# Moving the transpose of P behind the step's other queue entries, and loading wq in four column parts, in a causal attention plus mixture-of-experts kernel

## The reference

```
h = layernorm(x)
q, k, v = split(h @ W + b)            # W: 1024 x 3072
x = x + softmax(mask(q @ k.T / 32)) @ v
h = layernorm(x)
p = softmax(h @ router_w); keep the two largest of 8 as c
routed = sum_e c_e * (silu(h @ w1[e]) @ w2[e])
shared = sigmoid(h @ gate_w) * ((silu(h @ Wg) * (h @ Wu)) @ Wd)
x = x + routed + shared
```

## Time and profile before

| | us |
|---|---|
| median of 2 runs | 2761.55 |
| the two runs | 2738.25 and 2784.85 |
| profiled execution, its time | 2776.87 |
| its span on the slowest core (core 3) | 2775.0 |
| spans of the 8 cores | 2720.0 to 2775.0 |
| TensorE busy | 2249.7 (81%) |
| Vector busy | 729.1 (26%) |
| Scalar busy | 708.7 (26%) |
| Scalar idle until a load of xkv lands | 384.5 |
| Vector idle until a load of xkv lands | 349.5 |

### The profile page before, as it was taken

The page is one execution under the profiler, slowest core; times in us unless marked ns, Lnnn a source line. Parts: engine busy times, 40 slices in busy tenths (PEclk is TensorE's granted clock), DMA queues, the critical chain, the costliest instruction groups (busy, mean ns, idle before and its releaser), DMA issues.

```text
span 2775.0 us, 26258 instructions; the slowest of 8 cores (2720.0 to 2775.0 us)
## 1 busy us (share of the span) xinstructions
PE 2249.7 (81%) x9600; PEld 954.8 (34%) x9600; DVE 729.1 (26%) x945; ACT 708.7 (26%) x1256; POOL 58.7 (2%) x190
## 2 busy tenths in 40 slices
PE   2529699789779688696859346689999999999999
PEld 0203244233234233232323112234444444444444
DVE  3422332331342332323332311120211202202112
ACT  3212322332232333334342332212011021120110
POOL 0000000000000000000000000000000000000000
PEclk8769899787789889787978578899999999999999
DMA  6471320320230321303241323200311131113013
GB/s 144 103 111 37 76 58 14 79 58 29 57 76 25 73 76 37 79 29 80 56 95 29 70 44 53 46 0 1 59 33 31 31 61 31 31 31 61 1 31 121
DMA packets 204062, 149.70 MB, mean 54 GB/s; under 512 B 176160, under 2 KB 176288, under 8 KB 203936
## 3 DMA queue, kind: packets, MB, share of 16 engines
q1 hardware_dynamic: 189872, 101.88, 14.8%
q0 software_dynamic: 14064, 46.16, 10.6%
HBM read 142.79 MB, written 8.39 MB: 54 GB/s over the span
## 4 chain that ended last, share of the span: by engine, by line
PE 66%; DMA 10%; ACT 7%; DVE 6%; SPq 5%; issue 3%; DVEq 2%; ACTq 2%
PE pO L893 16%; PE sp L872 16%; PE pO L536 9%; PE pO L505 9%; DMA xb<-xkv 6%; PE pO L417 3%; SPq L226 3%; PE sp L348 3%; DMA xb<-xq 3%; PE sp L792 2%; PE sp L797 2%; DVEq L51 2%; ACTq L51 2%; PE pO L263 2%; ACT P L390 2%
## 5 line engine op out<-in xcount | busy, mean ns | idle before, releaser
L348 PE MATMUL sp<-K_sb,Q_sb 128*128 128x512 bf16 x1088 | 317.0, 458 | 163.5 <-ACT P L390 152.4
L872 PE MATMUL sp<-Q_sb,w 128*128 128x512 bf16 x2048 | 443.3, 379 | 0.0
L893 PE MATMUL pO<-w_sb,hb 128*128 128x512 bf16 x2048 | 443.3, 379 | 0.0
L902 DVE SCALAR_TENSOR_TENSOR O<-pO,c_sb,O 128x1024 f32<-128x1024 f32 x128 | 164.3, 1284 | 719.7 <-PE pO L893 719.7
L417 PE MATMUL pO<-V_sb,PTd 128*128 128x512 bf16 x1088 | 275.6, 411 | 67.9 <-DMA PTd<-P 67.9
L880 ACT ACTIVATE hb<-sp 128x1024 bf16<-128x1024 f32 x128 | 131.2, 1025 | 752.8 <-PE sp L872 752.8
L505 PE MATMUL pO<-xlnT,wkv_sb 128*128 128x512 bf16 x1024 | 247.1, 408 | 61.9 <-DMA xlnT<-xlnb 56.9
L872 PEld LDWEIGHTS sp<-Q_sb,w 128*128 128x128 bf16 x2048 | 200.4, 98 | 241.6
L893 PEld LDWEIGHTS pO<-w_sb,hb 128*128 128x128 bf16 x2048 | 200.4, 98 | 241.6
L536 PE MATMUL pO<-wkv_sb,xlnT 128*128 128x512 bf16 x1024 | 250.0, 401 | 0.0
L348 PEld LDWEIGHTS sp<-K_sb,Q_sb 128*128 128x128 bf16 x1088 | 119.5, 113 | 357.9 <-issue 299.8
(11 more groups left out here) (81 smaller groups left out, 1040.4 us busy)
## 6 DMA issues: line engine op xcount, KB each, us to landing
xb<-xkv SPq DMA_DIRECT2D x64, 512.0 KB, 4.6
xb<-xq SPq DMA_DIRECT2D x32, 512.0 KB, 4.2
w<-w1p POOLq DMA_DIRECT2D x8, 2048.0 KB, 16.2
w_sb<-w2p POOLq DMA_DIRECT2D x8, 2048.0 KB, 16.3
out<-O SPq DMA_DIRECT2D x16, 512.0 KB, 2.7
wkv_sb<-wkvh POOLq DMA_DIRECT2D x2, 2048.0 KB, 29.5
wgu<-wguh POOLq DMA_DIRECT2D x16, 256.0 KB, 5.7
wq_sb<-wqh POOLq DMA_DIRECT2D x1, 2048.0 KB, 21.9
```

Source lines behind the costliest of these rows:

```text
L348: p.emit("tensor", lambda e, t=t, h=h, qc=qc, j=j: e.matmul(sp[j][:, h * 512:h * 512 + 512], Q_sb[:, qc * 2048 + t * 128: qc * 2048 + t * ...
L872: p.emit("tensor", lambda e, e_i=e_i, th=th, fc=fc, dc=dc, nbq=nbq, jj=jj: e.matmul(sp[jj][:, nbq * 512:nbq * 512 + 512], w1_sb[e_i % 2][: ...
L893: p.emit("tensor", lambda e, th=th, tc=tc, fc=fc, nbq=nbq: e.matmul(pO[tc % 2][:, nbq * 512:nbq * 512 + 512], hb[th][:, fc * 1024 + tc * 1 ...
L902: p.emit("vector", lambda e, tl=tl, tc=tc, e_i=e_i: e.scalar_tensor_tensor(out=O[tl][:], in0=pO[tc % 2][:], scalar=c_sb[:, tl * 8 + e_i: t ...
```

## The change

Two edits.

The first is in the tile loop. `emit_PdmaT` of tile i is no longer emitted right after `emit_exp` of tile i, but in step i+1, ahead of that step's `emit_softmax`. Only SP's list is affected. For the last tile of a block it is emitted behind the loop and the AV before the last.

The second loads wq as four DMAs, each with 256 of the 1024 columns of all eight 128-row chunks, each with its own semaphore; column groups 2w and 2w+1 of `emit_qproj` wait for part w alone. In the program's list the DMA is 128x4x2048 elements before (pieces of 4096 bytes in SBUF, which holds bf16) and four times 128x8x256 after (pieces of 512 bytes); the two loads of wkv are 128x8x1024 (2048 bytes).

```diff
-    WQ = mk("WQ"); WKV = mk("WKV"); WV = mk("WV"); RG = mk("RG"); DW = mk("DW")
+    WQ = [mk(f"WQ{i}") for i in range(4)]; WKV = mk("WKV"); WV = mk("WV"); RG = mk("RG"); DW = mk("DW")
...
-    p.emit("gpsimd", lambda e: e.dma_start(out=wq_sb[:], in_=wqh, max_dma_last_dim=8192),
-           inc=WQ, inc_n=16)
-    lw_wq = WQ.n
+    for wqq in range(4):
+        p.emit("gpsimd", lambda e, wqq=wqq: e.dma_start(
+            out=wq_sb[:].rearrange("p (dc n) -> p dc n", dc=DC)[:, :, wqq * 256:wqq * 256 + 256],
+            in_=wqh.rearrange("p (dc n) -> p dc n", dc=DC)[:, :, wqq * 256:wqq * 256 + 256],
+            max_dma_last_dim=8192), inc=WQ[wqq], inc_n=16)
     emit_memsets()
...
     def emit_qproj(g, trd_wait):
         nonlocal u
-        p.wait("tensor", WQ, lw_wq)
...
         for qc in range(8):
+            p.wait("tensor", WQ[qc // 2], 16)
             p.wait("tensor", SC, pO_free_sc[u % 2])
...
                 t_av = emit_AV(at, ah, ar, apte)
                 emit_Ofin(at, ah, ar, t_av, asc)
+            if pend:
+                pt_, ph, pr, psc, _ = pend[-1]
+                v_pte = emit_PdmaT(pt_, ph, pr, psc)
+                pend[-1] = (pt_, ph, pr, psc, v_pte)
             v_nmnew = emit_softmax(t, halves, masked, r, t_qk, sc_exp_parity[r % 2])
             sc_exp = emit_exp(t, halves, r, v_nmnew)
             sc_exp_parity[r % 2] = sc_exp
-            v_pte = emit_PdmaT(t, halves, r, sc_exp)
-            pend.append((t, halves, r, sc_exp, v_pte))
+            pend.append((t, halves, r, sc_exp, None))
...
-        pt_, ph, pr, psc, v_pte = pend[-1]
+        pt_, ph, pr, psc, _ = pend[-1]
+        v_pte = emit_PdmaT(pt_, ph, pr, psc)
         while qidx < n_kv_items:
             run_item(items[qidx]); qidx += 1
```

## The result

The changed kernel takes 2568.31 us (median of 11 runs) against 2784.1 for the kernel before (10 runs beside it). The ratio is 0.9322, with a 95% interval from 0.9262 to 0.9381: 6.8% faster, some 187 us of the 2761.55 that the prediction started from.

What follows compares the result with a forecast made beforehand. Attention was taken as bound by a ring: in-order SP held loads of x behind P transposes waiting for exp. Gains 124 + 28 + 17 + 7 = 176, less 17 and 4, took 2761.55 to about 2605 us; range 2565 to 2665.

Steps and rivals of the forecast that it cites:

- The ring over the load: Attention blocks 0 to 4: earlier loads of x let two tiles take 15.4 us; 24.8 us a block, 124 in all.
- The sum: Gains of 124 (blocks 0 to 4), 28 (xq loads), 17 (block 5) and 7 (block 6): 176 us.
- my net: Whole kernel: 176 us less 17 and less 4, a gain of 155 to 156 us.
- 4 for wq: Start of kernel: loading wq in short pieces delays the first projection, a loss of 4 us.
- the tenth: 17 us taken off the 176 for kvt issues of 2.1 us and QK at the lower clock after a pause.
- rival A: Attention: denser matmuls hold the clock at 0.81, costing 140 us; net gain 16, 2745 us; chance 0.07 in either form.
- p3: Blocks 1 to 4: xq loads no longer behind a transpose; 8 us in blocks 1 to 3, 4 in block 4, 28 total.
- rival C: Attention steps: P issued late behind kvt holds up exp, 5.3 us a step; 2920 us, or 2840 with half; chance 0.02.
- Two marks: Signs of being right: xkv loads at 2% or less of the chain; Scalar's 384.5 us idle before L172 more than halved.
- B: Blocks 0 to 4: ring only partly opened, 9.7 us a tile, 84 us instead of 124; 2643 us; chance 0.19.
- D: SP's queue order does nothing, since loads wait for a free xb buffer; 2760 us; chance 0.04.
- the forecast: Whole kernel: the median becomes about 2605 us; chance 0.68.

Runs made afterwards that it cites:

- e4: Kernel before, wq in one DMA, transpose of P moved behind kvt but still ahead of the load: 2738.86 us against 2790.95.
- e9: e5 with three entries a step once the key tiles are done, so the p3 entries are spread as before: 2528.16 us, ratio 0.9153.
- e1: Changed kernel with wq back in one DMA, so only the transpose of P moved: 2558.4 us against 2790.95, ratio 0.929.
- e2: Kernel before with only wq loaded in four column parts, transposes of P as before: 2799.71 us against 2790.95.
- e5: e1 with each key load split from its sums, sums taken one step later, more entries a step: 2593.43 us, ratio 0.922.
- e3: Changed kernel with wq laid out by column part, so its four DMAs move 4096-byte pieces in place of 512: 2567.99 us.
- e7: The edits of e5 and e6 together: median 2566.11 us, ratio 0.9163.
- e10: The edits of e9 and e6 together: 2530.05 us, ratio 0.912.
- e8: e1 with blocks 5 and 6 keeping the old order of the transposes of P: 2611.48 us, ratio 0.932.
- e6: e1 with phase q's factors and normalisation of tile i-1 emitted ahead of the square of tile i: median 2573.88 us, ratio 0.9127.

## Why the prediction was right, and where it was off

*The ring over the load* was right in place and size. Two tiles in 15.4 us was predicted, 15.4 and 15.6 were measured; e4 shows that with the load behind P the ring stays, and e9 that it opens fully when the load gets a step's time before its sum is taken.

*The sum.* Cores 0, 1, 6 and 7 have no long stretch at 0.81 in either profile, so they show the change without that level of the clock. They became faster by 184.9, 183.1, 181.0 and 180.2 us (2722.0, 2734.8, 2720.0, 2733.8 before). That is 182 on the mean, where my net was 155 and my 176 less 4 for wq is 172. On core 0, from the issue of load 3 to the three loads ahead of the next block, blocks 0 to 4 take 135.7, 133.2, 121.4, 108.3 and 112.3 us before and 112.7, 100.7, 86.5, 73.7 and 82.7 after:

| block | gain in the sum | measured on core 0 |
|---|---|---|
| 0 | 24.8 | 23.0 |
| 1 | 32.8 | 32.5 |
| 2 | 32.8 | 34.9 |
| 3 | 32.8 | 34.6 |
| 4 | 28.8 | 29.6 |
| 5 | 17 | 17.5 |

For block 5 the stretch is from the three loads to the next three, 140.4 and 122.9 us. Block 6, from its first kvt to its last P, took 50.3 us before on core 3. On core 0 it took 49.0 (1357.82 to 1406.84) and takes 41.1 (1185.42 to 1226.47), a gain of 8 where the sum had 7. The terms are right within about 2 us each, and together they gave 180 where the sum had 176.

*The step that failed is the tenth.* I took 17 us off for slow kvt issues and for QK at the lower clock. The first doesn't show in the step times of the table, and the second was taken with the wrong sign: with fewer pauses QK ran slowly less often (302.0 to 257.3 us on core 0, in the lines above). Of the 27 us that the 155 is short of 182, this is 17, the terms are 4 and wq, as told below, up to 4; the last 2 stay open. No run shows a price for either of the two reasons that I gave for the tenth.

*The clock went in the other direction from rival A.* Cores 2 and 3, granted 0.81 for part of attention in the profile before (core 3 in the V projection of the earlier trace rows), gained 229.8 and 227.6 us, some 46 more than those four, and have no long stretch at 0.81 after. Core 5, at 0.81 before too, held it after for part of block 0 (0.81 over 310 to 400 us) and gained 187. That the ratio's 187 is above the 182 of the four cores fits this, but isn't shown by itself. So 0.81 came and went between executions on changing pairs of cores; e4 had it on cores 0, 1, 6 and 7. Denser attention alone doesn't bring it on: the profiles of the changed kernel and e1 are denser and have less of it. With one profile each it isn't shown that it became rarer, and what brings it on stays open. The Trainium skill's rule ("TensorE: Matmul & The Clock Gate", warning on the peak-current limiter), by which a whole die falls to 13/16 of the clock once three of its cores run dense matmuls, isn't what these profiles show: after the change all eight cores are dense in the expert stage, and each was granted 1.00 over 1827 to 2500 us.

*p3* behaved as worked out: tiles 5 and 7 are 18.8 us apart (538.99 to 557.83), 18.1 expected, 22.1 before.

*wq.* A loss of 4 was expected at the first projection; 0.0 to 4.7 was measured, by core (38.03 to 38.57 before, 38.26 to 42.98 after). I carried it to the end, and on most cores it didn't get there: the first load in the tile loop of block 0 is issued 1.1 us earlier to 0.7 us later than before on six cores. On cores 4 and 5 it is 10 us later (280.31 to 290.08 and 278.60 to 288.50). Whether wq did that isn't shown, since in e2 the same load moves by -4.5 to +4.4 us. Its lower bound, a gain, is excluded by e2.

*Late transposes of P (rival C)* exist where I put them. In blocks 5 and 6 Scalar's corr waits 9.1 us in all for them, 4.35 of it just ahead of the last tile of block 6, inside the 3 to 5 that I gave. Made worse in e5, they ate a gain of some 35 us, the difference between e5's and e9's spans.

*Two marks that I had set were missed.* The loads' share of the chain was to fall to 2% or less, and it is 4%. Scalar's idle time before the square was to fall by more than half, from 384.5; it is 264.9. The first I should have seen: a ring that still runs over the load keeps the load on the path, once for two tiles. The second holds seven waits of about 30 us, one under each V projection (31.7 the longest, 211.5 in all), where Scalar has nothing else to do and nothing waits for it. They were there before too, 220.4 us in all, so what the change could reach fell from 164 to 53 us. It was a bad mark for this change.

*The rivals.* The slow ring of B (9.7 us a tile) isn't there: 31.8 us for four steps is 7.95 a tile. D falls with the result. The chances were added wrongly: the forecast, B and half of A make 0.905 and not 0.92, and D with the other half of A 0.075 and not 0.06.

## What to carry to other kernels

On a queue that is issued strictly in order, look at what a transfer stands behind, not only at what it waits for: a load whose buffer is free but that follows an entry waiting for compute belongs ahead of it. When such a ring is opened, write down the next one (here normalised tile, kvt, load, sum ahead of maximum) with its time and the number of tiles it covers; that gave 15.4 us before the run, and the fix for it (e9) afterwards. And when entries of a schedule are regrouped, check for each waiting entry which of its neighbours it now stands behind, since e5 lost its whole gain to that alone.

## What was not expected of the hardware

Cast DMAs from GpSimd with 512-byte pieces landed in 22.4 us a part, with 4096-byte pieces in 15.6, four of each in flight. Yet the SP traffic beside the short pieces wasn't served better than beside one DMA of long pieces: on core 5 of the changed kernel one transpose took 5.78 us to issue, in the earlier trace rows 4.86. Beside four DMAs of long pieces (e3) the same transpose took 1.7 to 2.3 us on the eight cores. There it was issued some 2 us later, when less of wq was left, so this doesn't show that the number of DMAs helps.

In the profiles long stretches with a granted clock of 0.81 appeared on cores 2 to 5 before, on 4 and 5 after, in e2 on 0 to 5, in e4 on 0, 1, 6 and 7, in e7 and e10 on 2 and 3, in e8 on 0 and 1, and on none in e1, e3, e5, e6 and e9, each time in attention and not in the dense expert matmuls (1.00 over 873 us in the earlier trace rows). Their cause wasn't tried.
